# VectorE's order in the odd steps of layer 0's attention: the later chunk's row maxima ahead of the subtraction

## The reference

```python
q = jnp.einsum('bsm,hmd->bhsd', x, kernel[0])
k = jnp.einsum('bsm,hmd->bhsd', x, kernel[1])
v = jnp.einsum('bsm,hmd->bhsd', x, kernel[2])
scale = jnp.float32(1.0 / (d * d * h))
scores = jnp.einsum('bhsd,bhtd->bhst', q, k) * scale
attn = jax.nn.softmax(scores, axis=-1)
out = jnp.einsum('bhst,bhtd->bhsd', attn, v)
...
x = x + s * g
```

## Time and profile before

| what | us |
|---|---|
| median of 3 runs | 3077.13 |
| lowest and highest run | 3074.41, 3077.42 |
| profiled execution, its own time | 3079.59 |
| span of that execution in the trace | 3077.9 |
| busy PE, DVE, ACT, POOL in the span | 2807.8, 2504.0, 1557.4, 2502.6 |

### The profile page before, as it was taken

How to read it: one execution, slowest core, us unless ns; L and a number is a source line. 1 busy time by engine, 2 the same in 40 slices (tenths; PEclk the granted TensorE clock), 3 DMA queues, 4 the chain that set the end, 5 groups by cost and what they waited for, 6 DMA issues and landing times. The chain is left out here.

```text
span 3077.9 us, 46733 instructions
## 1 busy us (share of the span) xinstructions
PE 2807.8 (91%) x17656; PEld 1147.6 (37%) x17656; DVE 2504.0 (81%) x3379; ACT 1557.4 (51%) x1889; POOL 2502.6 (81%) x1205
## 2 busy tenths in 40 slices
PE   5959999999999999996499599999999999999997
PEld 3413333333333333333354133333333333333332
DVE  6568888888888888874339699999999999999995
ACT  4325555555555555552122255555555555555554
POOL 0009999999999999994339389999999999999997
PEclk9979999999999999997699699999999999999998
DMA  4250111111111111101203501111111111111100
GB/s 109 86 191 22 35 29 28 28 28 28 28 28 28 28 29 28 28 1 38 60 27 137 190 4 52 55 55 55 55 55 55 55 55 55 55 55 55 55 1 14
DMA packets 63825, 155.28 MB, mean 50 GB/s; under 512 B 18017, under 2 KB 33770, under 8 KB 61426
## 3 DMA queue, kind: packets, MB, share of 16 engines
q1 hardware_dynamic: 62578, 150.20, 17.4%
q0 software_dynamic: 1024, 2.10, 0.2%
HBM read 113.34 MB, written 38.93 MB: 49 GB/s over the span
## 5 line engine op out<-in xcount | busy, mean ns | idle before, releaser
L943 POOL TENSOR_TENSOR a_sums<-a_sums,room 128x1024 f32<-128x1024 f32 x512 | 1195.4, 2364 | 83.1 <-ACT room L795 42.5
L699 PE MATMUL a_ov<-room,va 128*64 128x512 f32 x4096 | 994.0, 606 | 0.0
L784 ACT ACTIVATE room<-room,sscale 128x1024 f32<-128x1024 f32 x512 | 588.3, 1149 | 539.3 <-DVE room L878 539.2
L845 DVE TENSOR_REDUCE a_mx<-a_jb 128x1 f32<-128x1024 f32 x501 | 611.9, 1221 | 129.6 <-PE a_jb L653 123.4
L943 POOL TENSOR_TENSOR a_sums<-room 128x1024 f32<-128x1024 f32 x256 | 604.3, 2361 | 116.6 <-ACT room L784 66.8
L840 DVE CUSTOM_DVE_ANT_0 a_junk<-a_jb,a_tab 128x1024 bf16<-128x1024 f32 x501 | 610.5, 1219 | 83.2 <-PE a_jb L653 74.8
L878 DVE TENSOR_TENSOR room<-a_st,a_tab 128x1024 f32<-128x1024 f32 x512 | 622.9, 1217 | 12.4 <-PE a_st L688 10.2
L795 ACT ACTIVATE room<-a_st,sscale 128x1024 f32<-128x1024 f32 x256 | 285.3, 1114 | 360.1 <-PE a_st L688 360.1
L652 PE MATMUL a_jb<-a_kh,a_qh 64*128 64x512 f16 x1002 | 384.9, 384 | 66.1 <-DVE a_mx L840 32.1
L699 PEld LDWEIGHTS a_ov<-room,va 128*64 128x64 f32 x4096 | 248.7, 136 | 409.3 <-issue 372.7
L688 PE MATMUL a_st<-a_qh,a_kh 64*128 64x512 f16 x2048 | 395.6, 383 | 3.0 <-DVE a_mx L840 2.9
(11 more groups left out here) (219 smaller groups left out, 2642.6 us busy)
## 6 DMA issues: line engine op xcount, KB each, us to landing
a_tab<-bias_line SPq DMA_DIRECT2D x16, 1984.0 KB, 11.0
qk_high<-q_oh SPq DMA_DIRECT2D x32, 512.0 KB, 2.6
qk_low<-q_ol SPq DMA_DIRECT2D x32, 512.0 KB, 3.6
a_qh<-qk_high SPq DMA_DIRECT2D x64, 256.0 KB, 4.5
a_kh<-qk_high SPq DMA_DIRECT2D x64, 256.0 KB, 5.1
a_ql<-qk_low SPq DMA_DIRECT2D x64, 256.0 KB, 7.5
a_kl<-qk_low SPq DMA_DIRECT2D x64, 256.0 KB, 7.8
ex_w<-in_L_ffn_W SPq DMA_DIRECT2D x1, 2048.0 KB, 10.5
```

The costliest lines, as they stand in the source:

```text
L699: last = nc.tensor.matmul(ov[t * DH:(t + 1) * DH, :], k.va[:, 2 * s + t, h * DH:(h + 1) * DH], prob[:, step % RING, t * QC:(t + 1) * QC], ...
L784: nc.scalar.activation(prob[:, r, :], prob[:, r, :], ACT.Exp, scale=k.sscale[:, layer:layer + 1])\
L845: nc.vector.reduce_max(mx[:, j // 2, j % 2:j % 2 + 1], scratch(n, j), AX.X).then_inc(max_done, 1)
L943: nc.gpsimd.tensor_tensor(a, first, prob[:, step % RING, :], ALU.add).then_inc(summed, 1)
```

## The change

In VectorE's loop the call of `maxima` is moved ahead of the call of `subtract_maxima`. In an even step of layer 0, and in all steps of layer 1, `subtract_maxima` is not called and the order stays. In an odd step of layer 0 the order was subtraction of step s, maxima tile s of chunk n + 2; now it is the maxima tile, then the subtraction. No instruction is added or removed and no wait is added to one; the other engines' lists are as before.

```diff
                 for s in range(NS):
                     if bias:
                         add_bias(n, s)
+                    if n + AHEAD < NCH:
+                        maxima(n + AHEAD, s)
                     if not by_row(NS * n + s):
                         subtract_maxima(n, s)
-                    if n + AHEAD < NCH:
-                        maxima(n + AHEAD, s)
                     if s == sum_step and n >= 1:
                         invert(n - 1)
```

## The result

The changed kernel takes 3191.62 us (median of 4 runs, 3186.36 to 3193.72) against 3075.78 us of the kernel before (median of 4 runs): a ratio of 1.0374, 95% interval 1.0356 to 1.0392. It is 116 us slower, more than twice the 52 us of the forecast and above its range. It went rival A's way: the stall was there as worked out, and in most chunks it took TensorE's clock down.

A forecast was written before the change was run, and what follows sets the result against it. TensorE and GpSimd were taken as near their limit, in loops of almost equal pace. Sixty periods each 0.84 us longer give 50.4 us, with the ends +52 us: 3077.1 + 52 = 3129 us, range 3105 to 3165.

The forecast's parts named there:

- rival A: TensorE's stall ahead of sums_of takes its clock down: 3227 us if every stall does, 3162 if a third; chance 0.20.
- What bounds the kernel now: Layer 0's attention: TensorE 98% and GpSimd 95% busy; GpSimd's loop has only 0.13 us slack under the 18.62 us period.
- The two loops of 18.62 and 18.49 us: Per chunk: TensorE's loop with its odd-reduction wait, 18.62 us; GpSimd's loop through four engines to sums_of, 18.49 us.
- The change part by part: Layer 0's odd steps: reduction done 0.91 us earlier, subtraction 1.37 us later; chunk period grows 0.84 us to 19.46.
- the add of step 5: GpSimd's add in pair 2 must wait for exponential 5 until 5.80 us after the pair's start, almost 1 us.
- Who waits for that: Users of the later odd exponentials: TensorE's values, the st buffer and even reductions covered, GpSimd's adds not.
- The price of one fall: TensorE behind sums_of at the lower clock: 1.21 us to the next pair plus some 0.4 on the scores, 1.6 us.
- B: At step 5's add, the earlier maxima tile wins and GpSimd keeps 18.49 us: 3069 us; chance 0.06.
- C: Exponential 5 only 0.41 to 0.54 us later, GpSimd's loop at 18.62 us, nothing measurable changes: 3077 us; chance 0.04.
- D: Only exponential 7 delays GpSimd: loop 19.13 us, 0.51 us a chunk, +31 us, 3108 us; chance 0.07.

The follow-up runs named there:

- e7: The kernel before, with layer 0's sums_of moved behind the values of its pair on TensorE: 3071.92 us, ratio 0.9988.
- e5: The kernel before, with the new VectorE order in step 1 of each chunk alone: 3068.45 us, ratio 0.9978.
- e1: The changed kernel, with five useless matmuls of 384 columns ahead of layer 0's sums_of: 3129.53 us, ratio 1.0174 to the kernel before.
- e2: The changed kernel, with layer 0's sums_of moved behind the values of its pair: 3073.36 us, ratio 0.9992 to the kernel before.
- e8: The changed kernel, with layer 0's sums_of behind its pair's values and ScalarE's output copy moved behind exponential 0: 3054.16 us, ratio 0.9929 to the kernel before.
- e9: The kernel before, VectorE's order unchanged, with an extra 512-column add on GpSimd ahead of layer 0's fold: 3197.53 us, ratio 1.0393.
- e3: The kernel before, with the new VectorE order in step 5 of each chunk alone: 3130.06 us, ratio 1.0177.
- e4: The kernel before, with the new VectorE order in step 7 of each chunk alone: 3112.65 us, ratio 1.0122.

## Why the prediction was wrong

*What bounds the kernel now* held. The two loops of 18.62 and 18.49 us are both seen, the first in e7 and the second in e5.

*The change part by part* held to the new period. The earlier tile, the subtraction 1.37 us later, the add of step 5 as the one that waits, the new period (19.46 worked out, 19.445 measured) and the idle time of about 1.05 us (measured 1.05) are all in the trace after. With the stall filled, e1 takes what the forecast said: 3129.5 us for 3129. One wait was missed in *Who waits for that*: the values of pair 1 also need ScalarE's copy behind exponential 1. In the changed kernel the stall hides it; in e2 it costs the 0.30 us that e8 wins back.

*The choice between the forecast and rival A* is the step that failed. The text had the idle time, 1.05 us, and the one row near it, 1.11 us in chunk 62 with a fall behind it; the row without a fall, 0.46 us, was far off. By the nearest row the falls were the likely case. I gave them 0.20, on the argument that chunk 62 without maxima tiles is a lighter chunk. That argument was never held against a row, and it does not hold: the changed kernel's chunks and e9's are full ones, and the clock fell in them. So the forecast put at nothing a term that measured 59 us. And the range took in falls in about a third of the chunks at most; it was 36 of 61. The price of one fall was right: 1.6 us, measured 1.645, though its parts were not (1.21 and 0.4 us, the second a guess). In the rows of after it is 0.89 us up to the next pair 2 (718.50 to 722.24, 3.74 us instead of the 2.85 from 699.06 to 701.91) and some 0.75 on the scores behind (722.24 to the add at 728.76, 6.52 us, instead of the 5.77 from 701.91 to 707.68). The granted clock gives nearly the same price: in the three stretches of 2 us from 719 to 725 it was 0.85, 0.50 and 0.80, which is 0.3 + 1.0 + 0.4 = 1.7 us of full-speed time lost. With 36 falls in place of none the same sum gives 3129 + 59 = 3188, against 3191.6.

The Trainium skill, page "TensorE: Matmul & The Clock Gate", section "A second HAM failure mode: psum-queue depth-cycling", was named for rival A: short idle times that come again and again make the clock go back and forth. Here the trace agrees, with 36 falls behind stalls of about 1.05 us, one in each round, and a mean clock of 0.95. Stalls of 0.86 us, just as frequent, brought one fall, at the start of the stage (e3).

*Rivals B, C and D*: B's wait and its gain exist, but only where step 1 alone is changed (e5, 8 us faster). D is e4, 19.18 us for the 19.13 worked out. Neither decides while step 5 is late.

What stays open: why, of 61 stalls, nearly all of about 1.05 us, 36 were followed by a fall and 25 were not. The runs show that it is so in two kernels with different orders (36 and 27 falls), and that the falls come in a regular order: in the first 42 stalls of the changed kernel no two stalls without a fall stand side by side, and single falls and pairs of falls follow each other almost in turn. What decides, beside the length of the stall, no run took apart.

## What to carry to other kernels

When an edit makes the busiest engine wait once in every round of a loop, work out two prices: the wait, and what the clock does behind it. If the expected idle time is about as long as one in the trace that was followed by a fall, take falls for the likely case, and look for the work that can fill the gap or be moved ahead of the wait.

A gain on one engine is stopped at the next loop's pace, here after 0.13 us; find that loop first. It may be quicker to move the one instruction that waits for the slow loop behind other work (e2), and then the next wait (e8), than to speed anything up.

## What the runs showed of the hardware that was not expected

Once per round, a little more idle time made the difference between no falls and many: 0.86 us of idle time ahead of sums_of, once per chunk of about 19.4 us, left TensorE at 2.4 GHz in 60 of 61 periods, and 1.05 us took it to 1.2 GHz in 36 of 61. Some 0.2 us more idle time thus came with 59 us more over the stage. Single stalls do not follow this order: at the start of the stage the clock fell after 0.96 us (e5) and stayed up after 1.58 us (e4) and 1.70 us (e9). And useless matmuls in the idle time paid for themselves: five more in each chunk made the changed kernel 62 us faster (3191.6 to 3129.5).
